# A local-attention and gated-FFN layer on eight cores: the order of two vector-engine steps per attention stage, and one input load in one piece instead of two

## The reference, cut to what matters

```python
q = x @ q_w.T                      # 16 heads of 64
k, v = split(x @ kv_w.T)           # one k and one v head, shared by the 16
attn = softmax(q k^T * SCALE)      # within blocks of 256 tokens
x = layernorm(x + (attn v) @ proj_w.T + proj_b)
h = silu(x @ wg.T) * (x @ wu.T)    # 1024 -> 3072, int8 weights / 127
x = layernorm(x + h @ wd.T)        # 3072 -> 1024
```

## Time and profile before

| what | value |
|---|---|
| median of 3 runs | 979.79 us (978.72 to 1037.48) |
| the profiled execution | 977.76 us |
| its span on the slowest core (core 6) | 975.8 us |
| spans of the 8 cores | 966.0 to 975.8 us |
| PE busy | 807.8 us (83%) |
| DVE busy | 320.6 us (33%) |
| ACT busy | 240.0 us (25%) |
| mean granted TensorE clock, core 6 | 0.909 |

### The profile page before, as it was taken

The page is one execution under the profiler, slowest core; times in us unless marked ns, Lnnn a source line. Parts: engine busy times, 40 slices in busy tenths (PEclk is TensorE's granted clock), DMA queues, the critical chain, the costliest instruction groups (busy, mean ns, idle before and its releaser), DMA issues.

```text
span 975.8 us, 12560 instructions; the slowest of 8 cores (966.0 to 975.8 us)
## 1 busy us (share of the span) xinstructions
PE 807.8 (83%) x4214; PEld 356.6 (37%) x4288; DVE 320.6 (33%) x538; ACT 240.0 (25%) x745; POOL 119.3 (12%) x233
## 2 busy tenths in 40 slices
PE   7757776668989999847888899776798989999996
PEld 6123333223434444312333344332343444443332
DVE  0157775332122111112555455533212221111111
ACT  0055553212131111003333343421212111111111
POOL 3000100002222233100000010000122223310000
PEclk9578888789999999956999899689899999999999
DMA  8951110234444455541111130112443444531221
GB/s 117 270 137 23 16 51 24 74 97 151 141 119 141 131 149 152 105 84 43 44 44 44 45 87 33 44 65 97 141 139 118 143 140 151 151 97 40 74 71 65
DMA packets 46973, 94.15 MB, mean 96 GB/s; under 512 B 5568, under 2 KB 5568, under 8 KB 46912
## 3 DMA queue, kind: packets, MB, share of 16 engines
q0 software_dynamic: 37536, 67.91, 27.0%
q1 hardware_dynamic: 9376, 25.43, 7.7%
HBM read 63.44 MB, written 12.58 MB: 78 GB/s over the span
## 4 chain that ended last, share of the span: by engine, by line
PE 63%; DMA 13%; DVE 8%; issue 8%; ACT 6%; POOL 0%; SPq 0%; DVEq 0%; ACTq 0%; POOLq 0%
PE ps L268 60%; DMA wqsb<-wq 5%; DMA x<-xtm 4%; PE ps L385 3%; ACT pool L353 2%; DMA xbf<-xfm 2%; DVE silu L714 2%; DVE pool L393 2%; DMA wuw<-wu 1%; ACT r L722 1%; DVE r L714 1%; ACT silu L722 1%; DVE x2s L732 1%; DVE xbf L460 1%; DVE hbuf L598 1%
## 5 line engine op out<-in xcount | busy, mean ns | idle before, releaser
L268 PE MATMUL ps<-xbf,wgw 128*128 128x512 bf16 x754 | 182.9, 384 | 17.6 <-DVE xbf L460 16.8
L268 PE MATMUL ps<-xbf,wuw 128*128 128x512 bf16 x750 | 183.2, 384 | 12.8 <-DVE hbuf L598 11.1
L268 PE MATMUL ps<-wdres,hbuf 128*128 128x512 bf16 x744 | 184.0, 390 | 10.3 <-issue 1.4
L598 DVE SCALAR_TENSOR_TENSOR hbuf<-ps,silu 128x512 bf16<-128x512 f32 x96 | 66.4, 692 | 268.4 <-PE ps L268 264.1
L353 ACT ACTIVATE pool<-ps 128x256 bf16<-128x256 f32 x256 | 97.9, 383 | 120.2 <-PE ps L268 95.2
L593 ACT ACTIVATE silu<-ps 128x512 f32<-128x512 f32 x96 | 56.9, 597 | 276.1 <-PE ps L268 276.0
L268 PEld LDWEIGHTS ps<-xbf,wgw 128*128 128x128 bf16 x768 | 75.2, 99 | 110.1 <-issue 23.9
L268 PEld LDWEIGHTS ps<-xbf,wuw 128*128 128x128 bf16 x768 | 75.2, 99 | 106.4 <-issue 19.3
L268 PEld LDWEIGHTS ps<-wdres,hbuf 128*128 128x128 bf16 x768 | 70.9, 99 | 114.2 <-issue 45.4
L568 POOL DMA_DIRECT2D wgw<-wg x96 | 51.1, 532 | 342.7 <-PE ps L268 342.7
L268 PE MATMUL ps<-xbf,wqsb 128*128 128x512 bf16 x247 | 77.5, 455 | 9.5 <-DMA wqsb<-wq 4.0
(11 more groups left out here) (56 smaller groups left out, 350.9 us busy)
## 6 DMA issues: line engine op xcount, KB each, us to landing
wgw<-wg POOLq DMA_DIRECT2D x96, 256.0 KB, 2.6
wuw<-wu POOLq DMA_DIRECT2D x96, 256.0 KB, 2.6
x<-xtm SPq DMA_DIRECT2D x16, 512.0 KB, 3.9
y<-x SPq DMA_DIRECT2D x16, 512.0 KB, 2.9
wdres<-wd POOLq DMA_DIRECT2D x1, 6144.0 KB, 49.2
wqsb<-wq POOLq DMA_DIRECT2D x18, 256.0 KB, 3.9
x2scr<-x2s SPq DMA_DIRECT2D x16, 256.0 KB, 2.2
x2s<-x2scr SPq DMA_DIRECT2D x16, 256.0 KB, 3.3
```

Of the source, the lines that this page charges most:

```text
L268: last = t.matmul(o, l, r, start=st_, stop=sp, tile_position=tpos)
L598: return v.scalar_tensor_tensor(H_sb[:, m, n * 512:(n + 1) * 512], bank(6)[:, 0:512], FS, silu_sb[:, par, n * 512:(n + 1) * 512], ALU.mult ...
```

## The change

It does two things. In `chain_stages` the block of `emit_AT` is written ahead of the block of `emit_norm`. And the first load of `xbf` is one DMA of 1024 rows (2 MB in SBUF) on semaphore xc0, in place of two of 512 rows on xc0 and xc1; all eight K/V operations of either token half now wait for that one DMA.

```diff
-        P.dma("gd", "xc0", lambda g: g.dma_start(
-            xbf_sb[:, 0:4, :],
-            xfm_d[0:512, 0:ST].rearrange("(k p) t -> p k t", p=128)),
-            reads=(), writes=XC[0:4], note="ld xbf st0 lo")
-        P.dma("gd", "xc1", lambda g: g.dma_start(
-            xbf_sb[:, 4:8, :],
-            xfm_d[512:1024, 0:ST].rearrange("(k p) t -> p k t", p=128)),
-            reads=(), writes=XC[4:8], note="ld xbf st0 hi")
+            xbf_sb[:, :, :],
+            xfm_d[:, 0:ST].rearrange("(k p) t -> p k t", p=128)),
+            reads=(), writes=XC, note="ld xbf st0")
...
                         emit_S(st, j, b, bm)
                         if j + 1 < NPAIR and b == 0:
                             emit_wq(st, j + 1)
+                    if 2 <= i <= NCH + 1:
+                        j, b = divmod(i - 2, NBLK)
+                        emit_AT(j, b)
                     if 1 <= i <= NCH:
                         j, b = divmod(i - 1, NBLK)
                         emit_norm(j, b)
-                    if 2 <= i <= NCH + 1:
-                        j, b = divmod(i - 2, NBLK)
-                        emit_AT(j, b)
```

## The result

The changed kernel takes 1000.38 us in the median of 8 runs (994.82 to 1003.04), the kernel before 979.47 (10 runs). The ratio is 1.0209, with a 95% interval of 1.0183 to 1.0234: slower by 20.5 us, clear of what the measurement is uncertain by and on the border of 2%. In some executions the cores of one die run at a lower clock and take some per cent longer, and the ratios here leave those out. The profiled execution has a span of 996.6 us on core 4, and all 8 cores are slower (987.5 to 996.6 us).

The account below looks back on a forecast made before the run. It took a loop between DVE and PE to bound the chain of half 0. Its terms, 7.9 + 2.5 + 3.4 + 0 + 3.5 = 17.3 us, on 977.76 gave 995.1, a median near 997, range 987 to 1008.

Parts of the forecast that it names:

- Step 1: Chain stages that nothing else covers: a DVE-PE loop of 2.97 us per stage, 3.39 at half the TensorE clock.
- Steps 2 and 3: Half 0: two longer loops in each of six pairs plus a later evacuation, 7.9 us; its uncovered end, 2.5 us.
- Step 4: Half 1: nothing beside the down matmuls; 3.4 us for the uncovered loops of j = 7 at half clock.
- Step 5: Start: merged load ends K/V 3.6 us later, hidden in PE's 4.03 us wait for Q weights; cost 0, bounds 0 to 3.6.
- The rival that the split load is worth its head start: Start: if the Q weights arrive sooner, up to 3.6 us show, giving 998 to 1001; chance 0.06.
- Step 6: TensorE's clock in half 0: added idle time ahead of its fall costs 3.5 us, bounds 0 and 12.
- The rival of a faster kernel: Half 0: copy first frees bank 7 earlier, 15 waits each 0.60 shorter, 9 us, so 970; chance 0.04.

Follow-up runs that it names:

- the filled kernels: Useless matmuls put into PE's waits of half 0: with the stage order of before, ratio 0.9913 to the kernel before; with the new order and split load, 1.0071.
- order_b01: Kernel before with the copy first only in half 0's stages of b0 and b1, pairs j = 1 to 6: ratio 1.0115.
- order_b23: Kernel before with the copy first only in half 0's stages of b2 and b3, pairs j = 1 to 6: ratio 1.0025.
- order_half1: Kernel before with the new stage order in half 1 alone, load still in two pieces: ratio 1.0014, 985.1 us.
- order_only: Kernel before with the new stage order in both halves, load still in two pieces: ratio 1.0196, 1001.3 us.
- noreload_merge: Kernel before without the second load of the j = 1 Q weights and with the input load in one piece: ratio 0.9995, 980.3 us.
- merge_only: Kernel before with only the input load merged into one piece, old stage order: ratio 1.0016, 984.3 us.

## Why the prediction was right

A median near 997 was forecast (987 to 1008), 1000.38 measured: a loss of 20.5 us where 17.3 were worked out. The mechanism was right, and one term was too small. By its steps:

- **Step 1 held to the hundredth.** The loop was worked out as 2.97 and 3.39 us; the trace has 2.96 to 2.98 and 3.36 to 3.39.
- **Steps 2 and 3 held.** 7.9 + 2.5 = 10.4 us were forecast for the chain of half 0 without the clock; the filled kernels differ by 10.3. Two readings in them were off without harm. The projection starts 0.67 us after the cast, not 1.05 (the missing record), and it does so in both kernels. And copy and multiply change places 62 times, in 31 stages of each half, not 64. order_b01 and order_b23 show that the loss sits in the stages of b0 and b1.
- **Step 4 held.** 3.4 us forecast, 3.2 in the changed kernel and 3.4 in order_half1 (2.6 in order_only). Beside the down matmuls nothing moved, even where 0.08 us were to spare.
- **Step 5 held, with less room than it seemed.** The load moved K/V by 3.3 us where 3.6 had been worked out, and the second load of the Q weights hid it. The wait of 4.03 was read some 0.4 us too long and the shift was worked out 0.3 too long, so it is partly luck that the 0.4 forecast to be left agree with the 0.20 measured. In the mean of the eight cores the cover (3.0 us) is no longer than the shift (3.2), and up to 0.7 us of cost in stretch 1 can't be told from the spread. noreload_merge shows what cover it was. The rival that the split load is worth its head start is true of a kernel without that cover.
- **Step 6 was mis-sized.** I took 3.5 us, between 0 and 12; it is 7.3 to 7.8. I took 0.5 for each pair, after the transposes of one loop at half clock (0.42), and 0.5 for the end of the half. A pair costs 0.94, and the end some 1.6: 0.8 up to the last cast (12.50 - 9.19, less 11.74 - 9.20 with the waits filled) and 0.8 from there to the first layer norm (7.61 us in place of 6.76, where the filled kernels have 7.08 and 7.06). What I had not counted is what runs at half clock behind the transposes. Core 4 has all records; before:

```profile
84.01 0.61 PE L385 MATMUL ps<-identB,pool 128*128 128x128 bf16 x8 [1.76 <-DVE pool L393]
...
84.89 3.19 PE L268 MATMUL ps<-xbf,wqsb 128*128 128x512 bf16 x8
```

And changed:

```profile
72.66 1.01 PE L381 MATMUL ps<-identB,pool 128*128 128x128 bf16 x8 [1.24 <-DVE pool L366]
...
74.17 3.59 PE L264 MATMUL ps<-xbf,wqsb 128*128 128x512 bf16 x8
```

From the transposes of b0 to the Q matmuls it is 0.88 us before (so in 30 of 36 pairs on the six cores with all records) and 1.51 after (in all 36): transposes and AV matmuls run at half. The scores do so too (87.10, 0.61 us in place of 0.40), and so do the projection's first matmuls. That the clock falls a stage earlier had been forecast. That it falls once in each pair, as the prediction says of the kernel before, is true of 42 of 48.

The sum of what was found is 10.3 + 7.3 + 3.2 = 20.8 us, against 20.5 measured. The first two add up to the 17.6 us of stretch 2 by the way they were taken; the 0.3 are what the other three stretches differ by. The rival of a faster kernel fell at the place that the prediction named: the copy's input is ready too late for the copy to be worth putting first (the sums of b3 at 80.68, the transposes of b2 done at 83.23).

On the clock, none of the waits that were filled was longer than 1.8 us, and filling them took it from 0.88 to 0.97. The rule of the Trainium skill that the prediction had weighed asks that TensorE not stand idle for long between bursts of matmuls (TensorE: Matmul & The Clock Gate, Why this matters for your kernels). Both kernels keep to it from one pair to the next, and the clock falls all the same, so the rule is not enough here.

## What to carry to other kernels

Two steps of one engine that feed the same consumer in turn should stand in the order in which their inputs come, not in the order of the chunks: with the later input first, its wait is added to the chain wherever the consumer has no other work. Before such a swap, write down the loop from one group of the consumer to the next with its latencies; a few rows of the trace gave the part of the loss that isn't clock to 0.1 us. And price the idle time that a new wait makes on TensorE at the clock too, over everything that runs behind it: here that was 0.7 us for each us of the loops themselves (7.3 to 10.3). And compare the count of a row with what the program writes before its start is read: where the first record is missing, as in three rows of before, start and wait are off by 0.4 us.

## What the runs showed of the hardware

- Matmuls without use in two waits of 0.95 to 1.8 us in each pair make the kernel 0.9% faster: the clock in the chain of half 0 goes from 0.88 to 0.97. They cost 0.08 us a pair (11.92 against 11.84 us at full clock).
- The matmuls that wait for an input load of 2 MB in one DMA start when those behind the second of two halves of 1 MB did (23.3 and 23.2 us on the cores shown; in the mean of eight cores 23.4 and 23.2, and 24.4 in merge_only beside 23.8 in order_only); POOL spent 0.89 us on its issue against 0.77 + 0.76 on two.
- The cores of one execution of before take from 251 to 261 us for stretch 3, with equal instructions; the effects here, of 3 to 20 us, could only be placed by means over all eight.
